# Attention on one Trainium2 core: small sums and multiplies moved from VectorE to GpSimd

## The chip, the cores and the metric

The kernel runs on one core of a Trainium2 chip. The time is that of the whole program on the device, in microseconds (us). The engines are TensorE (PE; its weight loads are PEld), VectorE (DVE), ScalarE (ACT), GpSimd (POOL) and SyncE (SP), which here issues all the transfers (DMA).

## The reference

A layer of a transformer: a normalised input goes through causal attention and then through three blocks of two small linear layers. Masked scores are not left out of the softmax: they count as 1e-10.

```python
x = L0_attn_residual                       # (2, 2048, 256)
# attention of layernorm(x): N = 16 heads, H = 64
scores = einsum('bknh,bqnh->bnqk', keys, queries) / sqrt(H)
scores = where(q_idx < k_idx, 1e-10, scores)
probs = softmax(scores, axis=3)
weighted = einsum('bnqk,bknh->bqnh', probs, values)
x = x + einsum('bqnh,nhe->bqe', weighted, W_output) + Bias_output
# then three times: linear (int4 and low rank), layernorm, gelu, linear, add
x = x + ffn(layernorm(x))
```

## The kernel before, in words

There are three stages with a barrier between them: normalisation and weights, attention, and the feed-forward stage. The change is in attention (function `attention`). Its outer loop runs over N = 16 pairs of heads (two batches, eight pairs each), numbered i = 0 to 15. In a pair the 2048 queries are cut into four groups of 512, worked in the order 3, 2, 1, 0, and a group's keys into tiles of two blocks of 128: NT = 20 tiles in a pair. Group 3 has tiles 0 to 7, group 2 has 8 to 13, group 1 has 14 to 17, group 0 has 18 and 19. For a tile TensorE computes the scores of both heads (`scores`, L822 and L824), ScalarE their exponentials (L961, to `probs`), and TensorE the products with the values (`weighted`, L843, to the PSUM bank `ps_o`). A tile is cut into six slots; between them TensorE does the background work of the next pair: projections (L757), score maxima (L766), and transposes. So 120 slots make a pair (`SLOTS`), and tables of slot numbers say what comes where. Each engine follows its own program in order, and semaphores hold them together.

How a group is finished:
- GpSimd adds up `probs` over the tiles of groups 3, 2 and 1 (`acc`, L724 for a group's first tile, L731 for the others), except in the last pair, where VectorE does that (L1071, L1077). TensorE sums `acc` over the keys with a matrix of ones; ScalarE copies the result to `den_rows` (L926).
- SyncE moves it to 32 partitions (`take_den`, L555, to `den_sq`). VectorE adds the masked keys' part (L1043, `total`) and inverts it (L1047, `inverse`): together they are `invert`.
- SyncE stores the inverse (`put_inverse`, L561) and loads it back spread over the partitions (`spread_inverse`, L570, to `scale`, two transfers).
- GpSimd makes the masked keys' part of the numerator (`masked_part`, L703), VectorE adds it to `ps_o` (`take_numerator`, L1035, to `num`) and multiplies with `scale` (`normalise`, L1055, to `o_out`). SyncE stores the result (`store_heads`, L576).

`num`, `scale` and `o_out` have two buffers, chosen by `group % 2`; `total`, `inverse` and `den_sq` have one. A numerator therefore waits for the multiply that read its buffer before, and TensorE's first product of a group waits for the numerator of the group before:

```python
                    if n >= 2:
                        dve.wait_ge(o_ready, START + n - 1)       # take_numerator
...
                            pe.wait_ge(num_ready, START + 4 * i + (3 - group))   # weighted, first tile of a group
```

Here `n = nth(i, group) = 4 * i + 3 - group` counts the groups. SyncE's queue is written out by hand. It also keeps and installs the split queries and keys of the next pair (`keep_split` L499, `install_chunk` L510, five transfers a chunk) and its maxima (`keep_max` L515, `keep_masked` L531, `install_max` L520). In the stretches below, pair 7 runs from about 1008 to 1127 us, pair 8 follows it, and pair 15 (the last) starts at 1955 us.

## Time and profile before

| | |
|---|---|
| median of 3 runs | 2433.36 us (2431.68 to 2435.09) |
| the profiled execution's own time | 2423.18 us |
| its span, first to last instruction | 2421.4 us |
| mean granted TensorE clock | 0.968 |
| busy: TensorE | 2247.3 us, 93% |
| VectorE | 1421.2 us, 59% |
| GpSimd | 1240.8 us, 51% |
| ScalarE | 813.6 us, 34% |

A busy share is taken over the whole span. An engine that is busy for half of it can still be waited for in one place of each pair, so the shares only say which engine could set the pace; the waits say where it doesn't.

### The profile page before, as it was taken

What the parts mean: (1) busy time and instruction counts of PE and PEld (TensorE: products, weight loads), DVE (VectorE), ACT (ScalarE), POOL (GpSimd) and SP (SyncE); (2) the same over time, 40 slices, a digit from 0 to 9 for tenths busy, and PEclk for the clock granted to TensorE, in tenths of its full rate; (3) what the DMA queues carried; (4) which work ended last, traced back from release to release, by engine and by line L of the source; (5) the groups of instructions that cost most, each with busy time, mean ns of one, the idle gap of its engine ahead of it and who ended that gap; (6) DMA issues with size and microseconds to landing.
All of it is one profiled execution on the core that took longest, in us unless ns stands there. A gap on an engine that the chain in (4) does not pass through costs nothing. (4 is left out here: it accounts for less than half of the span.)

```text
span 2421.4 us, 30652 instructions
## 1 busy us (share of the span) xinstructions
PE 2247.3 (93%) x10080; PEld 1149.0 (47%) x10080; DVE 1421.2 (59%) x3782; ACT 813.6 (34%) x1166; POOL 1240.8 (51%) x1139
## 2 busy tenths in 40 slices
PE   4389999999999999999999999999999995899987
PEld 3224444444444444444444444444444442767764
DVE  3585665656665656565656565656565763265664
ACT  1113434343434343434334344434343442011111
POOL 0106666667676757575757584858584810111110
PEclk8569999999999999999999999999999998899998
DMA  4564363635354445545453536353535332521100
GB/s 122 160 157 108 83 159 80 156 95 140 102 134 111 125 122 147 130 110 134 101 140 95 151 90 152 95 147 99 147 95 141 88 93 73 193 87 61 61 18 18
DMA packets 205356, 273.61 MB, mean 113 GB/s; under 512 B 69201, under 2 KB 86801, under 8 KB 205201
## 3 DMA queue, kind: packets, MB, share of 16 engines
q1 hardware_dynamic: 205200, 271.67, 42.8%
q8 instruction: 82, 1.34, 0.2%
q14 instruction: 74, 0.60, 0.1%
HBM read 176.69 MB, written 94.63 MB: 112 GB/s over the span
## 5 line engine op out<-in xcount | busy, mean ns | idle before, releaser
L731 POOL TENSOR_TENSOR acc<-acc,probs 128x512 f32<-128x512 f32 (+1 forms) x900 | 980.7, 1125 | 377.6 <-ACT probs L961 377.6
L961 ACT ACTIVATE probs<-ps_s 128x1024 f32<-128x1024 f32 (+2 forms) x640 | 549.4, 897 | 332.5 <-PE ps_s L824 157.2
L1011 DVE TENSOR_REDUCE partial<-ps_bg 128x1 f32<-128x512 f32 x768 | 490.3, 684 | 202.8 <-PE ps_bg L766 202.4
L822 PE MATMUL ps_s<-qq,kk 128*128 128x512 f32 (+3 forms) x1280 | 573.2, 448 | 18.8 <-ACT probs L961 18.8
L843 PE MATMUL ps_o<-probs,v 128*64 128x512 f32 (+3 forms) x2560 | 537.8, 541 | 0.0
L824 PE MATMUL ps_s<-qm,kl 128*128 128x512 f32 (+3 forms) x1280 | 467.1, 365 | 0.0
L757 PE MATMUL ps_bg<-xs,w_in 128*128 128x512 f32 x768 | 364.5, 599 | 20.8 <-DMA xs<-xn_turned 18.9
L822 PEld LDWEIGHTS ps_s<-qq,kk 128*128 128x128 f32 x1280 | 243.5, 190 | 202.4 <-issue 154.3
L766 PE MATMUL ps_bg<-k_bf,q_bf 64*128 64x512 bf16 (+3 forms) x1280 | 274.5, 364 | 20.2 <-DVE split L988 10.4
L1008 DVE CUSTOM_DVE_ANT_0 junk<-ps_bg,mask_q 128x512 bf16<-128x512 f32 (+3 forms) x512 | 230.7, 485 | 104.7 <-issue 103.5
L843 PEld LDWEIGHTS ps_o<-probs,v 128*64 128x64 f32 x2560 | 155.3, 136 | 229.9 <-issue 206.0
L824 PEld LDWEIGHTS ps_s<-qm,kl 128*128 128x128 f32 x1280 | 242.5, 189 | 38.8 <-issue 21.5
L766 PEld LDWEIGHTS ps_bg<-k_bf,q_bf 64*128 64x128 bf16 x1280 | 73.6, 93 | 355.0 <-issue 295.1
L910 ACT ACTIVATE split<-ps_bg,bias 128x512 fp32r<-128x512 f32 x128 | 88.0, 688 | 440.8 <-PE ps_bg L757 440.6
L724 POOL TENSOR_TENSOR acc<-probs 128x512 f32<-128x512 f32 x90 | 113.3, 1280 | 237.5 <-ACT probs L961 237.5
L988 DVE SCALAR_TENSOR_TENSOR split<-ps_bg,bias,split 128x512 fp32r<-128x512 f32 x128 | 94.6, 739 | 202.0 <-ACT split L910 201.3
L757 PEld LDWEIGHTS ps_bg<-xs,w_in 128*128 128x128 f32 x768 | 141.6, 191 | 131.0 <-issue 117.5
L1271 POOL TENSOR_TENSOR c_rstd<-c_var,c_minus_half 128x4 f32<-128x4 f32 x32 | 35.2, 1101 | 269.5 <-DVE c_var L1435 269.5
L1304 PE MATMUL c_ps<-c_wo,c_o_in 128*128 128x256 f32 x512 | 114.9, 384 | 28.5 <-DMA c_o_in<-heads_turned 28.5
L703 POOL TENSOR_TENSOR masked_num<-v_from,e 128x512 f32<-128x512 f32 x64 | 76.9, 1201 | 112.5 <-DVE num L1035 110.9
L1304 PEld LDWEIGHTS c_ps<-c_wo,c_o_in 128*128 128x128 f32 x512 | 98.7, 194 | 42.4 <-issue 28.7
L827 PE MATMUL ps_s<-never_above,ident_bf 128*128 128x128 bf16 x512 | 118.0, 230 | 0.0
(102 smaller groups left out, 1659.0 us busy)
## 6 DMA issues: line engine op xcount, KB each, us to landing
high_and_low<-split SPq DMA_DIRECT2D x128, 512.0 KB, 5.8
qq<-high_and_low SPq DMA_DIRECT2D x64, 512.0 KB, 4.7
kk<-high_and_low SPq DMA_DIRECT2D x128, 256.0 KB, 5.5
qm<-high_and_low SPq DMA_DIRECT2D x64, 256.0 KB, 6.4
kl<-high_and_low SPq DMA_DIRECT2D x64, 256.0 KB, 6.8
e<-masked_weights SPq DMA_DIRECT2D x128, 128.0 KB, 3.0
scale<-inverse_sums SPq DMA_DIRECT2D x128, 128.0 KB, 2.9
heads_turned<-o_out SPq DMA_DIRECT2D x64, 256.0 KB, 3.1
```

The source lines that it names most:

```text
L724: g.tensor_tensor(acc[h][:, group % 2, :], pr[:, 0:CH], pr[:, CH:2 * CH], ALU.add).then_inc(added, 1)
L731: g.tensor_tensor(acc[h][:, group % 2, q0:q0 + w], acc[h][:, group % 2, q0:q0 + w], probs[h][:, probs_slot(i, t), at:at + w], ALU.add).the ...
L757: mm = pe.matmul(bank("proj", j, u), w_in[:, s, m, :], xs[:, c, s, :], start=(s == 0), stop=(s == halves - 1))
L766: pe.matmul(bank("max", j, n, h)[:, 0:w], q_bf[HEAD[h], qb * P:(qb + 1) * P], k_bf[HEAD[h], CH * u:CH * u + w], start=True, stop=True).the ...
L822: pe.matmul(out, kk[:, h, kb * P:(kb + 1) * P], qq[:, h, q], start=True, stop=False, skip_group_check=True)
L824: mm = pe.matmul(out, kl[:, h, kb * P:(kb + 1) * P], qm[:, h, q], start=False, stop=not diagonal, skip_group_check=True)
L827: mm = pe.matmul(ps_s[:, h, at:at + P], ident_bf[:, :], never_above[:, :], start=False, stop=True, skip_group_check=True)
L843: mm = pe.matmul(ps_o[64 * h:64 * h + 64, q0:q0 + w], v[:, kb, 64 * h:64 * h + 64], probs[h][:, probs_slot(i, t), at:at + w], start=first, ...
L961: nc.scalar.activation(probs[h][:, probs_slot(i, t), 0:width], ps_s[:, h, 0:width], ACT.Exp, scale=SCORE_SCALE).then_inc(p_ready, 1)
L1008: e.tensor_tensor_reduce(junk[:, k, 0:w], of, mask_q[:, CH - w:CH], 1.0, 3 * NEVER, ALU.add, ALU.max, to).then_inc(max_read, 1)
L1011: e.reduce_max(to, of, AX.X).then_inc(max_read, 1)
L1304: mm = pe.matmul(ps_y[L][:, t, :], o_in[b][:, a, t * P:(t + 1) * P], wo[:, a, :], start=(a == 0 and t % 2 == 0), stop=(a == n_pairs - 1), ...
```

## The change

The sum (`total`) and the multiply (`o_out`) leave VectorE and become GpSimd's, in two functions `total_sum` and `normalise` with the same waits. GpSimd does them between its tiles, by the new tables `TOTAL_TILE` and `NORMAL_TILE`; an entry of NT or more is a tile of the next pair. VectorE keeps the reciprocal, at other slots. SyncE's queue is put in another order around them. The arithmetic is the same.

```diff
-INVERT_SLOT = {3: 68, 2: 106, 1: 118, 0: SLOTS + 8}
-NORMAL_SLOT = {3: 77, 2: 115, 1: SLOTS + 7, 0: SLOTS + 17}
+INVERT_SLOT = {3: 74, 2: 115, 1: SLOTS + 3, 0: SLOTS + 16}
+TOTAL_TILE = {3: 11, 2: 18, 1: NT, 0: NT + 2}
+NORMAL_TILE = {3: 14, 2: NT + 1, 1: NT + 2, 0: NT + 4}
...
+                def total_sum(i, group):
+
+                    n = nth(i, group)
+                    pool.wait_ge(den_sq_in, START + 32 * (n + 1))
+                    pool.wait_ge(masked_den_ready, START + i + 1)
+                    pool.wait_ge(inverse_ready, START + n)
+                    g.tensor_tensor(total[:, :, :], den_sq[:, :, :], masked_den[:, i % 2, group], ALU.add
+                                    ).then_inc(total_ready, 1)
+
+                def normalise(i, group):
+
+                    n = nth(i, group)
+                    pool.wait_ge(scale_in[group % 2], START + 32 * (2 * i + (3 - group) // 2 + 1))
+                    pool.wait_ge(num_ready, START + n + 1)
+                    pool.wait_ge(o_stored[group % 2], START + 16 * (2 * i + (3 - group) // 2))
+                    g.tensor_tensor(o_out[:, group % 2, :], num[:, group % 2, :], scale[:, group % 2, :], ALU.mult
+                                    ).then_inc(o_ready, 1)
+
+                def between_tiles(i, t):
+                    for c in (1, 0):
+                        if i and t == TOTAL_TILE[c] - NT:
+                            total_sum(i - 1, c)
+                    for c in (2, 1, 0):
+                        if i and t == NORMAL_TILE[c] - NT:
+                            normalise(i - 1, c)
+                    for c in (3, 2):
+                        if t == TOTAL_TILE[c]:
+                            total_sum(i, c)
+                    if t == NORMAL_TILE[3]:
+                        normalise(i, 3)
+                    for c in GROUPS:
+                        if t == MASKED_TILE[c]:
+                            masked_part(i, c)
...
                     for t in range(LAST_TILE[1] + 1):
                         group, tile = TILES[t]
-                        for c in (3, 2, 1):
-                            if t == MASKED_TILE[c]:
-                                masked_part(i, c)
+                        between_tiles(i, t)
...
-                    masked_part(i, 0)
-                masked_denominators(N - 1)
-                for c in GROUPS:
-                    masked_part(N - 1, c)
+                    between_tiles(i, LAST_TILE[1] + 1)
+                for t in range(NT):
+                    if t == MASKED_DEN_TILE:
+                        masked_denominators(N - 1)
+                    between_tiles(N - 1, t)
+                for t in range(NT, NT + 5):
+                    between_tiles(N, t - NT)
...
                 def invert(i, group):
 
                     n = nth(i, group)
-                    dve.wait_ge(den_sq_in, START + 32 * (n + 1))
-                    dve.wait_ge(masked_den_ready, START + i + 1)
-                    dve.wait_ge(inverse_ready, START + n)
-                    e.tensor_tensor(total[:, :, :], den_sq[:, :, :], masked_den[:, i % 2, group], ALU.add
-                                    ).then_inc(total_ready, 1)
                     dve.wait_ge(total_ready, START + n + 1)
                     dve.wait_ge(inverse_kept, START + 16 * n)
                     e.reciprocal(inverse[:, :, :], total[:, :, :]).then_inc(inverse_ready, 1)
...
-                normalise(N - 1, 1)
+                invert(N - 1, 1)
                 invert(N - 1, 0)
-                normalise(N - 1, 0)
```

VectorE where one pair ends and the next begins, before. The first row is the reciprocal's neighbour, the multiply of group 2; then come sum and reciprocal of group 1, the numerator of group 0, and the first projection reads of the next pair (`split0`).

```order
L1055 TENSOR_TENSOR o_out<-num,scale 128x512 [waits o_stored0,num_ready,scale_in0]
L1043 TENSOR_TENSOR total<-den_sq,masked_den 32x32 [waits inverse_ready,masked_den_ready,den_sq_in]
L1047 RECIPROCAL inverse<-total 32x32 [waits inverse_kept,total_ready]
L1035 TENSOR_TENSOR num<-ps_o,masked_num 128x512 [waits o_ready,masked_num_ready,pv_done]
L988 SCALAR_TENSOR_TENSOR split0<-ps_bg,bias,split0 128x512 [waits hi_ready]
L994 CAST q_bf<-split0 128x512
L988 SCALAR_TENSOR_TENSOR split0<-ps_bg,bias,split0 128x512 [waits hi_ready]
L996 CAST k_bf<-split0 128x512
```

The same place in the change; the first reciprocal is that of group 2, the second that of group 1.

```order
L1080 RECIPROCAL inverse<-total 32x32 [waits inverse_kept,total_ready]
L1073 TENSOR_TENSOR num<-ps_o,masked_num 128x512 [waits o_ready,masked_num_ready,pv_done]
L1026 SCALAR_TENSOR_TENSOR split0<-ps_bg,bias,split0 128x512 [waits hi_ready]
L1032 CAST q_bf<-split0 128x512
L1080 RECIPROCAL inverse<-total 32x32 [waits inverse_kept,total_ready]
L1026 SCALAR_TENSOR_TENSOR split0<-ps_bg,bias,split0 128x512 [waits hi_ready]
L1034 CAST k_bf<-split0 128x512
```

Each reciprocal has moved one place back in the chain of groups, the sum and the multiply are gone, and the numerator is now ahead of the reciprocal of group 1.

GpSimd at the same place in the change. The first two rows end a pair (the sum of group 2 and the masked part of group 0); the next four stand at tiles 0 and 1 of the next pair (the sum of group 1, the first additions, the multiply of group 2), then come the sum of group 0 and the multiply of group 1 at tile 2. Before, it had only the rows `masked_num` and `acc` here.

```order
L715 TENSOR_TENSOR total<-den_sq,masked_den 32x32
L706 TENSOR_TENSOR masked_num<-v_from,e 128x512
L715 TENSOR_TENSOR total<-den_sq,masked_den 32x32
L759 TENSOR_TENSOR acc<-probs 128x512 x2
L724 TENSOR_TENSOR o_out<-num,scale 128x512
L766 TENSOR_TENSOR acc<-acc,probs 128x512 x4
L715 TENSOR_TENSOR total<-den_sq,masked_den 32x32
L724 TENSOR_TENSOR o_out<-num,scale 128x512
L766 TENSOR_TENSOR acc<-acc,probs 128x512 x2
```

The sum of group 1 now stands ahead of the next pair's first additions, and the multiply of group 2 behind them.

SyncE over the same stretch, before. `den_sq` is `take_den` of group 1; the inverse behind it is that of group 1, and the five transfers from `high_and_low` ahead of it install chunk 1.

```order
L510 DMA qq<-high_and_low 128x2x512
L510 DMA kk<-high_and_low 64x2x512 x2
L510 DMA qm<-high_and_low 64x2x512
L510 DMA kl<-high_and_low 64x2x512
L555 DMA den_sq<-den_rows 32x1x16 x2
L576 DMA heads_turned<-o_out 128x512
L515 DMA maxima<-rows 8x128
L531 DMA masked_weights<-rows 8x128
L561 DMA inverse_sums<-inverse 32x2x16
L520 DMA qm<-maxima 1x2x512
L515 DMA maxima<-rows 8x128
L531 DMA masked_weights<-rows 8x128
```

The same stretch in the change. The inverse and the spread are those of group 2, `den_sq` is group 1's.

```order
L511 DMA qq<-high_and_low 128x2x512
L511 DMA kk<-high_and_low 64x2x512 x2
L511 DMA qm<-high_and_low 64x2x512
L511 DMA kl<-high_and_low 64x2x512
L516 DMA maxima<-rows 8x128
L532 DMA masked_weights<-rows 8x128
L562 DMA inverse_sums<-inverse 32x2x16
L571 DMA scale<-inverse_sums 64x512 x2
L556 DMA den_sq<-den_rows 32x1x16 x2
L521 DMA qm<-maxima 1x2x512
L516 DMA maxima<-rows 8x128
L532 DMA masked_weights<-rows 8x128
```

The denominators of group 1 have moved behind the maxima and masked weights of the next pair's group 1, and behind the inverse of group 2 and its spread, which stood ahead of the five transfers before.

## Rows read from the trace of the kernel before

**Rows 1.** The page, part 1: busy us, share of the span, instructions

```profile
PE 2247.3 (93%) x10080; PEld 1149.0 (47%) x10080; DVE 1421.2 (59%) x3782; ACT 813.6 (34%) x1166; POOL 1240.8 (51%) x1139
```

**Rows 2.** Chain of waits, TensorE, 297 to 1955: total us, times, longest

```profile
PE ps_s L822 <- ACT probs L961: 16.2, 14, 1.2
PE ps_bg L766 <- DVE split L988: 9.7, 14, 0.7
PE ps_bg L757 <- DVE split L988: 1.7, 5, 0.5
```

**Rows 3.** Timeline, ScalarE (start, us): first exponential of pairs 0, 1, 15

```profile
178.84 1.06 ACT L961 ACTIVATE probs<-ps_s 128x1024 f32<-128x1024 f32 x1
...
297.01 1.02 ACT L961 ACTIVATE probs<-ps_s 128x1024 f32<-128x1024 f32 x1
...
1955.47 1.02 ACT L961 ACTIVATE probs<-ps_s 128x1024 f32<-128x1024 f32 x1
```

**Rows 4.** Timeline, four engines, end of pair 7, start of 8; [idle before]

```profile
1123.59 0.40 ACT L935 ACTIVATE rows<-rows,masked_bias 8x128 f32<-8x128 f32 x1
...
1122.27 0.69 DVE L1055 TENSOR_TENSOR o_out<-num,scale 128x512 f32<-128x512 f32 x1
1129.26 0.79 DVE L1043 TENSOR_TENSOR total<-den_sq,masked_den 32x32 f32<-32x32 f32 x1 [6.30 <-DMA den_sq<-den_rows]
...
1130.36 0.62 DVE L1035 TENSOR_TENSOR num<-ps_o,masked_num 128x512 f32<-128x512 f32 x1
...
1131.74 0.42 DVE L994 CAST q_bf<-split 128x512 bf16<-128x512 f32 x1
...
1128.74 2.53 POOL L724 TENSOR_TENSOR acc<-probs 128x512 f32<-128x512 f32 x2 [9.51 <-ACT probs L961]
...
1133.79 1.51 PE L843 MATMUL ps_o<-probs,v 128*64 128x512 f32 x6
```

**Rows 5.** Timeline, SyncE's queue, the same place

```profile
1122.12 1.20 SPq L555 DMA_DIRECT2D den_sq<-den_rows  x2
...
1124.36 0.30 SPq L531 DMA_DIRECT2D masked_weights<-rows  x1
```

**Rows 6.** Timeline, SyncE's queue, end of the last pair

```profile
2026.66 0.31 SPq L561 DMA_DIRECT2D inverse_sums<-inverse  x1
2028.02 1.12 SPq L570 DMA_DIRECT2D scale<-inverse_sums  x2
2029.26 1.17 SPq L555 DMA_DIRECT2D den_sq<-den_rows  x2
```

**Rows 7.** The line L555 in the stretch 2026 to 2032

```profile
DMA to landing us min/median/max: 1.9/2.1/2.2
```

**Rows 8.** GpSimd by form, 297 to 1955: busy us, mean ns, idle before

```profile
L731 POOL TENSOR_TENSOR acc<-acc,probs 128x256 f32<-128x256 f32 x84 | 61.8, 757 | 0.0
L731 POOL TENSOR_TENSOR acc<-acc,probs 128x128 f32<-128x128 f32 x84 | 37.2, 465 | 0.0
```

**Rows 9.** Timeline, VectorE and TensorE, tile 2 of pair 8

```profile
1143.19 0.18 DVE L1043 TENSOR_TENSOR total<-den_sq,masked_den 32x32 f32<-32x32 f32 x1 [3.57 <-DMA den_sq<-den_rows]
...
1144.24 1.22 DVE L994 CAST q_bf<-split 128x512 bf16<-128x512 f32 x1
...
1144.37 1.98 PE L757 MATMUL ps_bg<-xs,w_in 128*128 128x512 f32 x4 [0.17 <-DVE split L988]
```

**Rows 10.** Timeline, TensorE, last pair: first product, and tile 5

```profile
1959.09 1.08 PE L843 MATMUL ps_o<-probs,v 128*64 128x512 f32 x4
...
1980.01 0.50 PE L822 MATMUL ps_s<-qq,kk 128*128 128x512 f32 x1 [1.02 <-ACT probs L961]
```

**Rows 11.** Timeline, SyncE's queue and VectorE, end of attention

```profile
2039.05 0.35 SPq L561 DMA_DIRECT2D inverse_sums<-inverse  x1
...
2045.01 0.34 SPq L576 DMA_DIRECT2D heads_turned<-o_out  x1
...
2044.28 0.69 DVE L1055 TENSOR_TENSOR o_out<-num,scale 128x512 f32<-128x512 f32 x1 [5.26 <-DMA scale<-inverse_sums]
```

More of the change, by code:

```diff
@@ L607, in _ @@
                     if i:
-                        spread_inverse(i - 1, 0)
+                        store_heads(i - 1, 1)
                     if more:
                         keep_split(i + 1, 2)
+                    if i:
+                        put_inverse(i - 1, 0)
+                        spread_inverse(i - 1, 0)
                     spread_masked(i, 2)
+                    if more:
+                        keep_split(i + 1, 1)
                     if i:
@@ L636, in _ @@
                         install_chunk(i + 1, 2)
+                    store_heads(i, 3)
+                    if more:
                         keep_max(i + 1, 2, fin_before(i, fin_index("mt", 2)) + 1)
@@ L641, in _ @@
                         install_max(i + 1, 2)
+                        install_chunk(i + 1, 1)
+                        keep_max(i + 1, 1, fin_before(i, fin_index("mt", 1)) + 1)
+                        keep_masked(i + 1, 1)
                     put_inverse(i, 2)
                     spread_inverse(i, 2)
[L644 to L645 removed]
                     take_den(i, 1)
[L647 to L651 removed]
                     if more:
@@ L1108, in _ @@
                                 invert(i - 1, g)
-                            if i and n == NORMAL_SLOT[g] - SLOTS:
-                                normalise(i - 1, g)
                         for g in GROUPS:
```

33 lines of the change are left out of this document (8 added, 25 removed).

## The prediction

> **What bounds the kernel now.** I read the page first: TensorE is busy 93% of the span [rows 1], and the part of the span in which it is not is mostly the first stage and the turn to the last one. The change is in the attention stage, so the next view is the chain of waits, cut to that stage: of some 1,658 us (pairs 1 to 14) TensorE waits 16.2 us for ScalarE's exponentials, 9.7 us for VectorE in front of a maxima product and 1.7 us for VectorE in front of a projection [rows 2]. The reader is to see two things there. First, TensorE sets the pace: whatever another engine saves is worth at most what TensorE waits for it. Second, the first two waits come 14 times each, once a pair, and are hand-overs TensorE, ScalarE, (VectorE), TensorE in which nothing of the change takes part. Then I took the length of a pair from ScalarE's timeline: pair 0 runs from 178.84 to 297.01, 118.17 us, and pairs 1 to 14 from 297.01 to 1955.47, 118.46 us each [rows 3]. Pair 0 has no earlier pair whose sums and divisions are finished in it; so what that finishing costs TensorE now is 118.46 - 118.17 = 0.29 us a pair.
>
> **Where the 0.29 us is.** In tile 2 VectorE waits 3.57 us for the denominators of group 0, adds them late, and only then reads the projection bank; TensorE's next projection waits for that read [rows 9]. The wait shown is 0.17 us in this pair; it is longer where the transfer is later.
>
> **The change, part by part.**
> (1) VectorE loses 64 sums and 64 multiplies. VectorE is idle before both now (6.30 us before the sum in [rows 4]), so the work saved is worth nothing by itself. What counts is that it no longer stands in a wait for a transfer at slot 8 of the pair: the bank read of tile 2 gets free. Worth up to 0.29 us, 14 times: -4.1 us. I take all of it, since the reciprocal stands at slot 16 now, behind the work that TensorE waits for. The other end is nothing, if the reciprocals wait for GpSimd instead.
>
> (2) GpSimd gains four sums and four multiplies a pair. They lie between its accumulations, and a late accumulation holds up ScalarE three tiles later, a long way off: GpSimd idles 9.51 us before it starts a pair [rows 4], and its extra work is some 4 x (0.35 + 1.26) = 6.4 us in 118. No term.
>
> (3) The new wait. The numerator of group 0, the last of a pair, goes to the buffer of group 2, so its instruction (L1035) waits until group 2 has been multiplied. Before, that multiply stood on VectorE at 1122.27, long done [rows 4]. Now it is GpSimd's, at tile 1 of the next pair, behind the sum for group 1 and behind the two additions of tile 0. TensorE's first product with the values in the new pair waits for this numerator, because it overwrites the PSUM bank, and it starts at 1133.79 now [rows 4]. Queued behind the numerator on VectorE are the first two projection reads. I follow the new chain in the times of that pair:
> - SyncE issues the inverse of group 2 behind the masked weights of group 1, which are ready at 1123.59 + 0.40 = 1123.99 [rows 4]; with that issue (about 0.4 us from one small one to the next) 1124.4 [rows 5]. The inverse itself has long been computed.
> - From that issue to the landing of group 1's denominators: the tail of the kernel has the same row of issues without anything else in flight. Inverse at 2026.66, two spreads from 2028.02, denominators at 2029.26 and about 2029.8 [rows 6], 1.9 to 2.2 us to land [rows 7], so 2031.8: 5.1 us. They land at 1129.5, near where they land now (1129.26 [rows 4]), since five large transfers no longer stand right ahead of them.
> - GpSimd's sum of 32x32 has no row. Below, the line through 757 ns for 256 columns and 465 ns for 128 [rows 8] gives 465 - 96 x 2.28 = 246 ns; above, it costs no more than 465 ns. I take 0.35: 1129.85.
> - Two additions, 2.53 us [rows 4]: 1132.4. Today they start at 1128.74; they can't before the sum now.
> - The multiply at the price of one such addition, 1.26 us: 1133.65. The numerator 0.62 us [rows 4]: 1134.3. Three hand-overs, 0.2 us in all: 1134.5.
> TensorE is ready at 1133.79, so it waits 0.7 us, at 14 boundaries: +9.8 us. The ends: sum at 0.25, the landing 0.2 earlier and no hand-over cost give 0.2 us; sum at 0.46 and the landing 0.5 later give 1.3 us. Times 14, +3 to +18.
>
> [...]
>
> (4) The last pair has no projections, so TensorE is at its first product already 3.6 us after the pair's start, at 1959.09 [rows 10]. Denominators land 2.8 us after the start (1955.47 [rows 3]), at 1958.3; sum 0.35, multiply 1.26 (no additions ahead of it, VectorE does them there), numerator 0.62, hand-overs 0.2: 1960.7, +1.6 us. Against it, TensorE waits 1.02 us in tile 5 today because VectorE's additions stood behind a wait for denominators and one for the inverse [rows 10]; both leave VectorE or come earlier: -1.0. Together +0.6.
>
> (5) The end of attention is a serial chain. The inverse of group 2 is issued 0.8 us later (2027.5 for 2026.66 [rows 6]), as its reciprocal now stands behind the numerator of group 1. Then 5.1 us to the next denominators, 0.35 + 1.26 + 0.62 + 0.34 for sum, multiply, numerator and reciprocal, with hand-overs 2035.3; the same 5.1 and 0.35 + 0.34 to 2041.1; from there to the last multiply 5.2 us (2039.05 to 2044.28 [rows 11]) and 1.26 for it: the last store at 2047.6 for 2045.01 [rows 11]. +2.6 us, and nothing hides it, since the last stage starts after it.
>
> **The sum:** -4.1 + 9.8 + 0.6 + 2.6 = +8.9 us, on the profiled execution's 2423.2 us: 2432.1. That execution lies 10.2 us under the median of the runs, 2433.36; the difference is added to the median: 2442.3, so 2442.
>
> **The rivals.**
> - *The new wait hides* (chance 0.14; the side that is not slower). If the numerator is done by 1133.79, that is if the chain is 0.7 us shorter than I make it, TensorE never waits. For it: the margin is small, and the chain was put together from rows of other places. Against: five of its links are rows, and it starts at a ScalarE instruction that the change can't move. Then -4.1 + 0.6 + 2.6 = -0.9 us: 2432, no change that can be measured. It decides at a landing of 1128.8.
> - *The chain is longer* (0.08): the spreads or denominators share their queues with the chunk's five transfers that follow, or the sum costs GpSimd 1 us. At 1.7 us a boundary, 14 x 1.0 more: 2456.
> - *VectorE and GpSimd get in each other's way* (0.05). VectorE's cast in tile 2 takes 1.22 us beside GpSimd's additions [rows 9] and 0.42 at 1131.74 [rows 4] without them, and its sum 0.79 us at 1129.26 beside them. Every multiply on GpSimd is a new stretch of this. If one of the four in a pair falls on a cast ahead of a read that TensorE waits for, 14 x 0.8 = 11 us more: 2453. The Trainium skill (SBUF — State Buffer, SBUF: two separate sides) says that the two share a port pair which one instruction holds to its end; by that rule it would be so, and these rows agree. But the multiplies at the boundary fall where VectorE stands still anyhow.
> - *VectorE's relief is worth more* (0.03): if it also ended the 9.7 us of [rows 2], about 2423. Against it: these waits come at one place in each pair, behind a projection that ScalarE has just read.
> - The forecast has what is left, 0.70.
>
> **The numbers.** With the forecast's ends (+3 to +18 for the boundary term, nothing to -4.1 for the first) its own range is 2435 to 2454. The range 2433 to 2456 leaves out most of the no-wait case (0.14) and the last rival, and takes in the longer ones. 0.2%, 4.9 us, is about what a measurement of this kernel can tell from no change. Slower by more than that: 0.64 of the forecast and the two longer cases, 0.77; within it: the hidden wait, and 0.05 of the forecast's lower edge, 0.19; faster, the last rival and a hundredth of the forecast, 0.04.
>
> **What would show it.** In the changed profile: the chain of waits has a new one, TensorE's product with the values (out ps_o) for VectorE's numerator, 15 times, 0.7 us each and 1.6 in the last pair. VectorE idles before the numerator until GpSimd's multiply. GpSimd's sum of 32x32 is at 0.25 to 0.46 us and starts 2.8 us after the pair's start. TensorE's waits for VectorE before a projection (1.7 us now) are gone. Pairs 1 to 14 are 118.9 us long. The last store is issued about 3 us later than now, counted from the last pair's start (89.54 us now [rows 3, 11]). I am wrong if the product with the values starts at once in a new pair; or if pairs lengthen with no wait at that product, which would speak for the shared port or a transfer.

## The result, and the profile after

| | before | changed |
|---|---|---|
| median, both timed side by side | 2434.23 us (4 runs, 2431.68 to 2444.36) | 2472.70 us (4 runs, 2466.16 to 2488.62) |
| profiled execution: span | 2421.4 us | 2476.6 us |
| pairs 1 to 14 in it | 1658.46 us | 1697.79 us |

The ratio is 1.016, with a 95% interval of 1.0099 to 1.022: slower, by 38.5 us, some four times the 8.9 us that were forecast (2442, range 2433 to 2456). The direction was right and the range too low.

The changed profile's page, engine line. GpSimd is busy for 1339.1 us where it was 1240.8, VectorE for 1393.0 where it was 1421.2; both have idle time to spare, so the shares explain nothing.

```profile
PE 2271.4 (92%) x10080; PEld 1163.5 (47%) x10080; DVE 1393.0 (56%) x3654; ACT 814.0 (33%) x1166; POOL 1339.1 (54%) x1267
```

ScalarE's timeline of the changed kernel at the starts of pairs 0, 1 and 15, as in [rows 3] (columns: start, duration, then what it is).

```profile
189.25 1.03 ACT L999 ACTIVATE probs<-ps_s 128x1024 f32<-128x1024 f32 x1
...
307.38 1.02 ACT L999 ACTIVATE probs<-ps_s 128x1024 f32<-128x1024 f32 x1
...
2005.17 1.02 ACT L999 ACTIVATE probs<-ps_s 128x1024 f32<-128x1024 f32 x1
```

The span grew by 55.2 us. The stage ahead of pair 0 took 10.4 us longer (189.25 for 178.84). That is not the change's: in the other profiles below, of either kernel, it begins at anything from 176.2 to 188.8. Pair 0, which finishes no earlier pair, is as long as before (118.13 us for 118.17). Pairs 1 to 14 are 39.3 us longer. The last store is issued 92.40 us after the start of pair 15, 2.9 later than before, and 2.6 us lie behind it. What lies behind the last store varies by as much among the profiles of this document (376.2 to 379.6 us). So I count 42 us as the change's. From ScalarE's exponentials one also reads each tile's length; over pairs 1 to 14 the mean changed so:

| tile | before, us | changed, us | times 14 |
|---|---|---|---|
| 1 | 7.61 | 8.36 | +10.5 |
| 2 | 4.73 | 4.47 | -3.6 |
| 3 | 10.30 | 12.03 | +24.2 |
| 4 | 7.99 | 8.19 | +2.9 |
| 5 | 5.26 | 5.59 | +4.6 |
| others | | | +0.8 |

Tile 3 is not a little longer everywhere: it is 10.30 us in nine of these pairs and 14.42, 17.27, 12.63, 14.66 and 16.69 us in pairs 3, 5, 8, 11 and 13. The same stretch in TensorE's waits of the changed kernel (waited for: us in total, times, longest), to be laid beside [rows 2]:

```profile
PE ps_bg L804 <- DVE split L1026: 9.7, 14, 0.7
PE ps_o L881 <- DVE num L1073: 9.5, 14, 1.2
PE ps_bg L795 <- DVE partial L1046: 9.4, 2, 4.7
PE ps_bg L804 <- DVE vt L1021: 6.0, 3, 2.2
PE ps_bg L804 <- DVE partial L1049: 4.5, 7, 1.0
PE ps_bg L804 <- DVE partial L1046: 2.0, 4, 0.6
```

The second row is the forecast wait for the numerator. The third and fourth were in nobody's list: two plus three waits in five pairs, for bank reads of VectorE that have nothing to do with the change. The fifth row lies in tile 5 of other pairs, and comes below. What VectorE did there, pair 5, timeline of VectorE and of GpSimd, with TensorE's wait:

```profile
806.12 0.75 DVE L1026 SCALAR_TENSOR_TENSOR split<-ps_bg,bias,split 128x512 fp32r<-128x512 f32 x1 [3.24 <-ACT split L948]
806.78 8.00 DVE L1032 CAST q_bf<-split 128x512 bf16<-128x512 f32 x1
814.71 0.68 DVE L1046 CUSTOM_DVE_ANT_0 junk<-ps_bg,mask_q 128x512 bf16<-128x512 f32 x1
...
806.48 0.24 POOL L715 TENSOR_TENSOR total<-den_sq,masked_den 32x32 f32<-32x32 f32 x1 [0.71 <-DMA den_sq<-den_rows]
806.69 1.26 POOL L724 TENSOR_TENSOR o_out<-num,scale 128x512 f32<-128x512 f32 x1
807.92 6.58 POOL L766 TENSOR_TENSOR acc<-acc,probs 128x512 f32<-128x512 f32 x8
...
815.45 2.08 PE L795 MATMUL ps_bg<-xs,w_in 128*128 128x512 f32 x2 [4.72 <-DVE partial L1046]
```

The cast shows as 8.00 us, as against 0.42 alone. It ends 0.3 us after GpSimd's row of ten instructions does (807.92 + 6.58 = 814.50), and behind it stand the reads that TensorE waits for. In pair 6 GpSimd paused 0.63 us between multiply and additions, and the same cast took 0.65:

```profile
932.13 0.24 POOL L715 TENSOR_TENSOR total<-den_sq,masked_den 32x32 f32<-32x32 f32 x1
932.34 1.28 POOL L724 TENSOR_TENSOR o_out<-num,scale 128x512 f32<-128x512 f32 x1
934.25 6.78 POOL L766 TENSOR_TENSOR acc<-acc,probs 128x512 f32<-128x512 f32 x8 [0.63 <-ACT probs L999]
...
933.26 0.65 DVE L1032 CAST q_bf<-split 128x512 bf16<-128x512 f32 x1
```

In the kernel before, no cast took more than 1.33 us: it waited for one GpSimd instruction at most. I call it a *hold* when a VectorE instruction stands through several.

Which of pairs 1 to 14 have one can be read off. In the five with a hold, the exponentials for which the additions wait end 0.22 to 1.30 us before the multiply ahead of them does, so the additions stand ready. In eight pairs they end after it, GpSimd pauses 0.09 to 0.63 us, and nothing is held. Pair 7 lies between: ready 0.13 us early (1052.34 + 1.71 = 1054.05, the multiply ends at 1054.18), no pause to be seen, and yet the cast gets in after one boundary:

```profile
1052.34 1.71 ACT L999 ACTIVATE probs<-ps_s 128x896 f32<-128x896 f32 x2
...
1053.14 1.33 DVE L1032 CAST q_bf<-split 128x512 bf16<-128x512 f32 x1
...
1052.71 0.24 POOL L715 TENSOR_TENSOR total<-den_sq,masked_den 32x32 f32<-32x32 f32 x1 [0.74 <-DMA den_sq<-den_rows]
1052.92 1.26 POOL L724 TENSOR_TENSOR o_out<-num,scale 128x512 f32<-128x512 f32 x1
1054.15 6.97 POOL L766 TENSOR_TENSOR acc<-acc,probs 128x512 f32<-128x512 f32 x8
```

A hold costs TensorE more than its wait. In tiles 3 and 4 the waits behind held casts sum to some 17 us (the third and fourth rows above, and 0.5 us each in tile 4 of pairs 3, 5 and 11), but the two tiles are 27.1 us longer. TensorE's granted clock, at its full level (1.0, 2.4 GHz) through pairs 1 to 14 of the kernel before, falls to the lower one (0.5, 1.2 GHz) in five stretches here, 20.5 us in all, in four of the five pairs with a hold. In pair 5 TensorE had stood still for all but 0.01 us of the 4.72 ahead of 815.45; in pair 11 for 2.21 us ahead of 1542.51. Two of the five stretches (columns: stretch, its length, busy time of PE, PEld, DVE, ACT and POOL, granted clock, DMA):

```profile
812.97:819.79 6.82, 4.34 (x8) 1.47 (x10) 4.56 (x10) 0.00 (x0) 1.52 (x4) 0.50 0.43 116
1543.42:1546.83 3.41, 3.41 (x7) 1.67 (x5) 0.88 (x7) 0.00 (x0) 0.00 (x0) 0.50 0.65 193
```

TensorE is busy for 17.6 of these 20.5 us. At full clock that work would take about half, so I estimate 8.8 us for the clock; about 1 of the 27.1 us is left over.

Tile 5 is another matter. It is at 5.26 or 5.27 us in the five pairs with a hold, and up to 6.29 in the others: there VectorE's cast waits for one GpSimd instruction, as in [rows 9], and TensorE's next maxima product waits for the reads behind it (the fifth row of the waits). In the kernel before that cast took 0.42 us in every pair; now the multiply of group 0 at tile 4 puts GpSimd's next instructions beside it (runs 14 and 15, with that multiply on GpSimd and no hold there, show the longer tile 5 too). Pair 6:

```profile
956.02 1.44 DVE L1032 CAST q_bf<-split 128x512 bf16<-128x512 f32 x1
...
955.90 1.27 POOL L706 TENSOR_TENSOR masked_num<-v_from,e 128x512 f32<-128x512 f32 x1
957.22 3.81 POOL L766 TENSOR_TENSOR acc<-acc,probs 128x512 f32<-128x512 f32 x3
```

The first account of the holds was: any longer unbroken run of GpSimd can hold a cast (theory A); the rival was a late transfer or the numerator's wait, carried on.

### The profile page after: what moved, and what is told of

The parts are those of the page before. It is cut to its first block and busy times, and to the rows that moved or that the text cites. A ratio compares the mean times of both kernels' runs of the same rounds, so it can differ in the third digit from the quotient of the medians.

```text
span 2476.6 us, 30652 instructions
## 1 busy us (share of the span) xinstructions
PE 2271.4 (92%) x10080; PEld 1163.5 (47%) x10080; DVE 1393.0 (56%) x3654; ACT 814.0 (33%) x1166; POOL 1339.1 (54%) x1267
## 3 DMA queue, kind: packets, MB, share of 16 engines
q8 instruction: 82, 1.34, 0.2%
## 5 line engine op out<-in xcount | busy, mean ns | idle before, releaser
L860 PE MATMUL ps_s<-qq,kk 128*128 128x512 f32 (+3 forms) x1280 | 574.2, 449 | 17.6 <-ACT probs L999 17.6
L795 PE MATMUL ps_bg<-xs,w_in 128*128 128x512 f32 x768 | 372.8, 611 | 27.9 <-DMA xs<-xn_turned 18.5
L804 PE MATMUL ps_bg<-k_bf,q_bf 64*128 64x512 bf16 (+3 forms) x1280 | 275.7, 364 | 33.1 <-DVE split L1026 10.4
L862 PEld LDWEIGHTS ps_s<-qm,kl 128*128 128x128 f32 x1280 | 242.6, 190 | 39.3 <-issue 22.1
L724 POOL TENSOR_TENSOR o_out<-num,scale 128x512 f32<-128x512 f32 x64 | 82.2, 1284 | 170.1 <-DMA scale<-inverse_sums 170.0
L1073 DVE TENSOR_TENSOR num<-ps_o,masked_num 128x512 f32<-128x512 f32 x64 | 43.9, 686 | 178.3 <-POOL o_out L724 171.6
L715 POOL TENSOR_TENSOR total<-den_sq,masked_den 32x32 f32<-32x32 f32 x64 | 15.7, 245 | 231.7 <-DMA den_sq<-den_rows 231.4
```

The costliest lines, as they stand in the source:

```text
L795: mm = pe.matmul(bank("proj", j, u), w_in[:, s, m, :], xs[:, c, s, :], start=(s == 0), stop=(s == halves - 1))
L804: pe.matmul(bank("max", j, n, h)[:, 0:w], q_bf[HEAD[h], qb * P:(qb + 1) * P], k_bf[HEAD[h], CH * u:CH * u + w], start=True, stop=True).the ...
L860: pe.matmul(out, kk[:, h, kb * P:(kb + 1) * P], qq[:, h, q], start=True, stop=False, skip_group_check=True)
L862: mm = pe.matmul(out, kl[:, h, kb * P:(kb + 1) * P], qm[:, h, q], start=False, stop=not diagonal, skip_group_check=True)
```

## The experiments

Pairs 1 to 14 are from the profiled execution of each; medians compare with the kernel before on the same chip. Runs 7 to 11, 16 and 17 were executed once each and the kernel of run 5 twice: for them the profile's tiles and casts count, not the time.

**1. Multiply of group 2 ahead of tile 0's additions.**

```diff
-NORMAL_TILE = {3: 14, 2: NT + 1, 1: NT + 2, 0: NT + 4}
+NORMAL_TILE = {3: 14, 2: NT, 1: NT + 2, 0: NT + 4}
```

> The changed kernel, but GpSimd multiplies group 2 ahead of its additions of tile 0 of the next pair instead of behind them (one entry of the table of multiplies, NT for NT + 1). Both theories agree on the first part: TensorE's wait at the first product with the values (for VectorE's numerator; 9.5 us over 14 pairs, longest 1.2) is gone or under 2 us, tile 1 of a pair is back from 8.34 to about 7.6 us. Theory A (most of the loss is VectorE's cast standing through a run of GpSimd instructions in tiles 2 and 3, 24 us in five of 14 pairs): the long tile 3 stays, pairs 1 to 14 are 10 us shorter, about 2463. Rival B (everything comes from the new wait, which delays what follows it): pairs 1 to 14 go back to 1660 us or so, 2435 to 2440.

Median 2483.27 us (before 2426.20), ratio 1.0235 (1.018 to 1.0289); pairs 1 to 14: 1711.3 us. Tile 1 is 7.61 us in all pairs: that wait was the multiply's place, as forecast. But holds of 4.1 to 8.2 us are now in 12 of 14 pairs. Rival B is out; A is right in kind and too small in size. More pairs are hit because in more of them the additions of tile 2 stand ready early: 0.32 to 1.40 us before the multiply ahead of them ends in the 12 pairs with a hold, 0.12 and 0.06 us in the two without. Here 41 us of pairs 1 to 14 are at the lower clock.

**2. The cast as another instruction.**

```diff
-e.tensor_copy(q_bf[:, cols(c)], part[:, 0, :].bitcast(F32))
+e.reduce_max(q_bf[:, cols(c)], part[:, 0, :].bitcast(F32).unsqueeze(2), AX.X)
```

> The changed kernel, but VectorE's two casts of the split queries and keys (0.42 us each when nothing disturbs them, 8.00 and 7.95 us in pairs 5 and 13 of the changed kernel, 4.2 to 4.6 in pairs 3, 8 and 11) are done by another instruction with the same result, a maximum over an axis of one element. Theory A (the cast is an instruction that needs something which GpSimd's additions hold, and it can stand through several of them): no such instruction takes over 1.3 us, tile 3 is back at 10.3 us in all pairs, tile 5 at 5.3; pairs 1 to 14 take 1697.8 - 24 - 4 = about 1670 us, with up to 5 us more if the other form itself costs 0.3 us at each of its 8 places; about 2445 us. Rival B (the long tiles come from late transfers that the cast only shows, since it stands behind them): the waits turn up on another instruction of VectorE and the time stays at 2465 to 2475.

Median 2444.69, ratio 1.0087 (1.0055 to 1.0118); pairs 1 to 14: 1676.5 us, tile 3 at 10.30 in all. VectorE's rows for the two casts as maxima (min/median/max ns): not one of 128 was touched (662 to 678 ns).

```profile
L1032 DVE TENSOR_REDUCE q_bf<-split x64: 674/676/678, 110.1 to 1892.9; 128x512 bf16<-128x512 f32 x64
L1034 DVE TENSOR_REDUCE k_bf<-split x64: 662/675/677, 111.4 to 1898.4; 128x512 bf16<-128x512 f32 x64
```

So the hold belongs to the instruction, not to what it waits for. The dearer form costs 0.26 us in each of tiles 4 and 5, the same in every pair: the single-boundary waits of tile 5 are gone too.

**3 and 4. One unused multiply put into the kernel before**, ahead of tile 2's additions, behind the wait for both exponentials (3) or for the first (4).

```diff
+if t == 2:
+    pool.wait_ge(p_ready, START + 2 * NT * i + 2 * t + 1)   # run 4; run 3 stands behind the full wait
+    g.tensor_tensor(idle_out[:, :], mask_q[:, :], mask_q[:, :], ALU.mult).then_inc(idle_done, 1)
```

> The kernel before with one instruction added on GpSimd in tile 2 of every pair but the last: a 128x512 multiply of constants whose result nobody uses (so the outputs are those of before). It stands behind GpSimd's wait for the exponentials of tile 2, directly ahead of the additions of that tile, and nothing else moves, no transfer either. Theory A1 (any longer back-to-back run of GpSimd can hold VectorE's cast for long): some casts over 2 us, TensorE stands in tile 3 of some pairs, pairs 1 to 14 longer by 3 to 25 us. Theory A2 (the cast is held only when GpSimd never stood still, that is when its additions were ready while the instruction ahead of them still ran): as the additions follow without a gap here too, a cast that begins beside this multiply can be held as well; one that begins later waits for one addition as before. Rival B (late transfers are the cause): nothing over 1.33 us, the time of before within 0.2%.

> The kernel before with the same unused 128x512 multiply on GpSimd in tile 2, but behind the first head's exponential of that tile alone, ahead of the wait for both heads: it starts some 0.5 us earlier, while the second head's exponential is still being computed, as the group's multiply often did in the changed kernel. Theory A (GpSimd's longer runs hold the cast): casts of 4 to 8 us in several of 14 pairs and a tile 3 of 12 us or more in these, pairs 1 to 14 longer by 10 to 30 us, about 2445 to 2460. Rival B (late transfers): no cast over 1.33 us, the time of before within 0.2%.

Ratios 1.0003 (0.9976 to 1.0029) and 1.0015 (0.9992 to 1.0038); no cast over 1.27 us. Theory A as stated falls: a longer unbroken run, as long as these, is not enough.

**5 and 6. A 32x32 sum and a multiply; two multiplies**, unused, at the same place.

```diff
+g.tensor_tensor(idle_sum[:, :, :], <32x32 of mask_q>, <32x32 of mask_q>, ALU.add).then_inc(idle_done, 1)   # run 5
+g.tensor_tensor(idle_out[:, 0, :], mask_q[:, :], mask_q[:, :], ALU.mult).then_inc(idle_done, 1)            # 5; twice in 6
```

> The kernel before with two unused instructions on GpSimd in tile 2 of every pair but the last, ahead of that tile's additions: a 32x32 sum and, straight behind it, a 128x512 multiply, of constants, into buffers that nobody reads. They start after the first head's exponential of the tile, so the additions follow without a gap, as in pairs 3, 5, 8, 11 and 13 of the changed kernel. Nothing else moves. The multiply alone at this place held no cast over 1.3 us. Theory A (it takes the small sum in front, or a run of at least two instructions in front of the additions): casts of 4 or 8 us in several pairs, tile 3 of 12 us or more there, pairs 1 to 14 longer by 10 to 35 us, 2435 to 2460. Rival B (the changed order of the transfers is needed as well): no cast over 1.6 us, the time of before within 0.2%.

> As the run with an unused sum and multiply, but with two unused 128x512 multiplies, no small sum: the same number of instructions in the run. Theory A3 (the number of instructions ready in a row counts): long casts as with sum and multiply. Theory A4 (the short instruction on 32 partitions counts, as the next instruction stands ready behind it at once): no cast over 1.6 us here. If neither this nor the run with the sum shows a long cast, both fall.

With the sum: ratio 1.0314 (1.0269 to 1.0359), pairs 1 to 14 at 1750.8 us, a hold in every one of pairs 0 to 14, and 79 us of pairs 1 to 14 at TensorE's lower clock. With two multiplies: 0.9993 (0.9967 to 1.0019), none. So SyncE's new order isn't needed for a hold, and at this place the sum is. In pair 4 of run 5 it is VectorE's own small sum that is held, 4.96 us for 0.18, until GpSimd has nothing more to do (689.35 + 4.37 = 693.72):

```profile
688.80 4.96 DVE L1054 TENSOR_TENSOR total<-den_sq,masked_den 32x32 f32<-32x32 f32 x1 [4.24 <-DMA den_sq<-den_rows]
...
688.14 0.24 POOL L722 TENSOR_TENSOR idle_sum<-mask_q 32x32 f32<-32x32 f32 x1 [1.23 <-ACT probs L972]
688.35 1.03 POOL L725 TENSOR_TENSOR idle_out<-mask_q 128x512 f32<-128x512 f32 x1
689.35 4.37 POOL L742 TENSOR_TENSOR acc<-acc,probs 128x512 f32<-128x512 f32 x4
```

**7 to 11. What it is about the sum.** Each is run 5 with its unused instructions changed. Run 7 has the sum alone, behind the wait for both exponentials; runs 8, 9 and 10 have these in place of the 32x32 sum; run 11 has the 32x32 sum alone, behind the first exponential, so that GpSimd then pauses for the second.

```diff
+g.tensor_tensor(idle_out[:, 1, 0:32], mask_q[:, 0:32], mask_q[:, 32:64], ALU.add)             # run 8, 128x32
+g.tensor_tensor(idle_out[0:32, 1, :], mask_q[0:32, :], mask_q[0:32, :], ALU.add)              # run 9, 32x512
+g.tensor_tensor(idle_out[0:64, 1, 0:32], mask_q[0:64, 0:32], mask_q[0:64, 32:64], ALU.add)    # run 10, 64x32
```

> The kernel before with one unused 32x32 sum on GpSimd, directly ahead of the additions of tile 2 and released with them, so that they follow it without a gap; no multiply. Theory A5 (the short instruction in front of a run is what makes the run hold VectorE to its end): long casts or a long sum of denominators on VectorE, 4 to 8 us, in several pairs; pairs 1 to 14 over 1680 us. Theory A6 (a short instruction and a long one must stand ahead of the additions): nothing over 1.6 us, pairs 1 to 14 at 1657 to 1662 us.

> As the run with an unused 32x32 sum and a multiply in the kernel before (which took 1751 us for pairs 1 to 14 and showed holds of 3.9 to 7.5 us in most pairs), but the sum is as short on all 128 partitions (128x32). If shortness is the cause, the holds stay, 1720 to 1770 us. If it is that the sum uses 32 partitions only, they vanish, 1657 to 1670 us.

> The opposite case: the sum is on 32 partitions but 512 elements long, some 1.0 us like the multiply behind it. If shortness is the cause of the holds: nothing over 1.6 us, pairs 1 to 14 at 1657 to 1670 us. If the use of 32 partitions is: holds in most pairs, over 1700 us.

> As the runs with an unused short sum and a multiply ahead of tile 2's additions in the kernel before, but the sum on 64 partitions. With 32 partitions pairs 1 to 14 took 1751 us, with 128 they took 1662. If every sum on fewer than all 128 partitions does it: over 1700 us and casts of 4 to 7 us; if 64 are enough to be harmless: 1657 to 1665.

> The kernel before with the one unused 32x32 sum, released by the first head's exponential of tile 2 and so ahead of the additions with a pause of some 0.4 us between them. The sum released with the additions, without a pause, held VectorE 3.7 to 6.8 us in 12 pairs and took 1728 us for pairs 1 to 14. If a moment in which GpSimd stands still undoes it: no cast over 1.6 us, 1657 to 1662 us. If not: over 1700.

| the unused instructions ahead of tile 2's additions | pairs 1 to 14, us | pairs of 0 to 14 with a VectorE cast or sum over 1.6 us (longest) |
|---|---|---|
| 32x32, multiply | 1750.8 | 15 (7.46) |
| 32x32 alone | 1727.9 | 15 (6.81) |
| 64x32, multiply | 1744.9 | 15 (7.69) |
| 128x32, multiply | 1661.9 | none |
| 32x512, multiply | 1671.6 | 5 (3.31) |
| 32x32, pause, additions | 1665.8 | none |
| two multiplies | 1667.2 | none |

Shortness alone is not it: 128x32 is as short (252 ns) and harmless. Using fewer than all partitions is, whether 32 or 64, and mostly when the instruction is short as well; with 512 elements the holds are few and end after two or three additions, which neither theory gave. A pause undoes it. The few us over 1658 of the harmless ones are in tile 2, where VectorE's sum waits for denominators that land later than before, and in some pairs for one GpSimd instruction (up to 1.16 us in all).

The kernel before has a GpSimd instruction on 32 partitions too (L694, 32x128, the fifth of its run). It says nothing either way: no cast or two-input sum of VectorE falls into the 4.9 us of the run behind it.

**12. The sum of the changed kernel on 128 partitions.** 96 of them hold a constant that nobody reads on, filled in once at the start.

```diff
-        total = sb("total", [32, 2, 16])     # den_sq and masked_den alike
+        total = sb("total", [P, 2, 16])
```

> The changed kernel with its sum of denominators done on 128 partitions instead of 32 (96 of them hold a constant that nobody reads on; the sum is as short, and no instruction, wait or transfer changes its place). Theory P (GpSimd's instruction on 32 partitions in front of its run is what holds VectorE): no cast over 1.6 us in tiles 2 and 3 of any pair, tile 3 at 10.3 us in all; the wait at the numerator stays (9.5 us over 14 pairs), so pairs 1 to 14 take 1697.8 - 24 to 28 = 1670 to 1674 us and the run about 2447. Rival (it is the place in the run or the changed order of transfers, and the unused instructions in the kernel before only happened to look alike): some pairs keep a tile 3 of 12 to 17 us, over 1685.

Median 2445.88, ratio 1.0049 (1.0027 to 1.0072); pairs 1 to 14 at 1677.7 us, tile 3 at 10.30 in all. VectorE's cast and GpSimd's run of pair 5, same place, same neighbours:

```profile
791.55 1.41 DVE L1034 CAST q_bf<-split 128x512 bf16<-128x512 f32 x1
...
791.19 0.25 POOL L717 TENSOR_TENSOR total<-den_sq,masked_den 128x32 f32<-128x32 f32 x1 [0.75 <-DMA den_sq<-den_rows]
791.40 1.28 POOL L726 TENSOR_TENSOR o_out<-num,scale 128x512 f32<-128x512 f32 x1
792.63 6.97 POOL L768 TENSOR_TENSOR acc<-acc,probs 128x512 f32<-128x512 f32 x8
```

The additions were ready 0.21 us early in this pair, which is next to the margin of pair 7 above; but they were 0.64, 0.84 and 1.27 us early in pairs 13, 8 and 3, and no cast of the run took over 1.52 us. This is the cause of the holds shown in the change itself. Against the changed kernel tiles 3 and 4 are 27 us shorter, but tile 1 is 4 us longer over 14 pairs (in pair 11 it takes 11.79 us: the numerator's longest wait, 2.4 us, and then 3.4 us at the lower clock), and tile 5 is 4 us longer, since more pairs reach it with the single-boundary wait. That is why the run is 4 us over the expectation.

**13. The same with run 1's table.**

> The same with the multiply of group 2 ahead of the additions of tile 0: both faults of the change mended, all sums and multiplies still on GpSimd at their tiles. Without the wide sum this order was the worse one (1711 us in pairs 1 to 14, long casts in 12 of 14). Theory P: tiles 1, 2, 3 at 7.61, 4.47, 10.3 us in every pair, some tenths lost in tile 5, pairs 1 to 14 at 1656 to 1661 us, about 2432 with the longer tail. Rival: over 1685.

Median 2433.07, ratio 0.9992 (0.9968 to 1.0016); pairs 1 to 14 at 1661.8 us. The order that was worst with a 32-partition sum is level with before when the sum is wide.

**14. The narrow sum moved to where GpSimd then pauses.**

```diff
-INVERT_SLOT = {3: 74, 2: 115, 1: SLOTS + 3, 0: SLOTS + 16}
-TOTAL_TILE = {3: 11, 2: 18, 1: NT, 0: NT + 2}
-NORMAL_TILE = {3: 14, 2: NT + 1, 1: NT + 2, 0: NT + 4}
+INVERT_SLOT = {3: 74, 2: 115, 1: SLOTS + 3, 0: SLOTS + 18}
+TOTAL_TILE = {3: 11, 2: 18, 1: NT, 0: NT + 4}
+NORMAL_TILE = {3: 14, 2: NT, 1: NT + 2, 0: NT + 5}
...
+                normalise(N - 1, 0)
```

> The changed kernel with GpSimd's work at other tiles: sum of group 0 ahead of tile 4 instead of tile 2 (there GpSimd then stands still), its reciprocal two slots later, its multiply at tile 5, and the multiply of group 2 ahead of the additions of tile 0. The multiply of group 1 stays ahead of tile 2's additions, now without a sum in front. Theory A (a short sum ahead of a long run is what costs): no cast over 1.6 us in tiles 2 and 3, tile 3 at 10.3 us, tile 1 at 7.6, tile 2 at 4.47; pairs 1 to 14 at 1655 to 1660 us; 5 us of the last pair and the tail remain, so 2425 to 2432, within 0.3% of before. Rival: the run moves elsewhere and holds another cast, over 1670 us in pairs 1 to 14.

Median 2430.91, ratio 1.0003 (0.998 to 1.0025); pairs 1 to 14 at 1661.8 us, no hold. Tile 5 is 5.77 us for 5.26 in each pair, behind the multiply of group 0.

**15. Only the multiplies on GpSimd**, the sum back in `invert`, at the changed slots.

```diff
 def invert(i, group):
+    e.tensor_tensor(total[:, :, :], den_sq[:, :, :], masked_den[:, i % 2, group], ALU.add).then_inc(total_ready, 1)
```

> The changed kernel with the sum of denominators back on VectorE, ahead of its reciprocal at the changed kernel's slots; the multiply stays on GpSimd and SyncE's order stays. Theory A4 (the small sum in GpSimd's run is needed for the long casts): no cast over 1.6 us, tile 3 at 10.3 us; the new wait at the first product with the values stays (9.5 us or somewhat less, as the multiply of group 2 no longer has a sum ahead of it, perhaps 3); pairs 1 to 14 at 1662 to 1672, total 2430 to 2440. Theory A3 (any longer run does it): with the multiply of group 1 still ahead of the additions of tile 2, long casts in some pairs, total over 2450. VectorE's sum for group 1 at slot 3 may wait for the denominators, at 2.8 us into the pair, and costs nothing there.

Median 2500.40, ratio 1.0254 (1.0216 to 1.0291), pairs 1 to 14 at 1724.1 us where I expected 1662 to 1672. Tiles 1, 2 and 3 are 7.61, 4.47, 10.30: no hold there. But tile 13 is 7.77 for 4.12 and tile 14 6.21 for 5.38. Of its VectorE sums one in each of pairs 0 to 14 (that of group 3) took 3.7 us:

```profile
L1066 DVE TENSOR_TENSOR total<-den_sq,masked_den x64: 154/174/3729, 270.4 to 2120.0; 32x32 f32<-32x32 f32 x64
```

No instruction on fewer partitions stands in GpSimd's run there. There is a second way into a hold.

**16 and 17. The kernel before, with that sum at the late slot; and a cast ahead of it.**

```diff
-INVERT_SLOT = {3: 68, 2: 106, 1: 118, 0: SLOTS + 8}
-NORMAL_SLOT = {3: 77, 2: 115, 1: SLOTS + 7, 0: SLOTS + 17}
+INVERT_SLOT = {3: 74, 2: 106, 1: 118, 0: SLOTS + 8}
+NORMAL_SLOT = {3: 86, 2: 115, 1: SLOTS + 7, 0: SLOTS + 17}
+                        if n == 68:                                     # run 17 alone
+                            e.tensor_copy(idle_bf[:, :], mask_q[:, :]).then_inc(idle_done, 1)
```

> The kernel before with sum and reciprocal of group 3 on VectorE at slot 74 instead of 68, where the run with the multiplies alone on GpSimd had them, and its multiply at slot 86 instead of 77, so that it doesn't wait for its transfer. GpSimd's program is untouched. In that other run this sum stood 3.73 us in every pair, until GpSimd's run ended, with no 32-partition instruction in the run since GpSimd last stood still; in the kernel before the same sum, six slots earlier in the same run, stood 1.10 us (to the next boundary). Theory L (it is enough that VectorE asks late in a long run, whose last stillness of GpSimd was some 19 us ago): the sum takes 3.7 us here too, tile 13 is about 7.7 us instead of 4.12, pairs 1 to 14 about 1708 us. Rival (GpSimd's changed program or the transfers made it so there): 0.4 to 1.3 us for the sum, pairs 1 to 14 at 1658 to 1662.

> The same, with one unused 128x512 cast on VectorE at slot 68, where the sum stood in the kernel before (its result is read by nobody). Theory L1 (the run of GpSimd gets out of step over time, and one VectorE instruction that gets in between two of its instructions puts it in step again): the unused cast takes 1 to 1.5 us and the sum at slot 74 no more than 1.3 us, pairs 1 to 14 at 1658 to 1665. Theory L2 (what stands nearest to the sum decides, whatever came before): the sum takes 3.7 us as in the run without the cast.

Run 16: pairs 1 to 14 at 1733.1 us, tile 13 at 7.70. That tile is as theory L said, the total 25 us over it: TensorE waits 2.66 us behind the held sum, then 3.4 or 6.8 us of every pair are at the lower clock, which reaches into tile 14 (6.53 us for 5.38), and tile 2 is longer too. VectorE and GpSimd in pair 7; GpSimd starts the run after a pause of 3.56 us, and 19 us later its 16th instruction since is under way:

```profile
1137.02 3.73 DVE L1043 TENSOR_TENSOR total<-den_sq,masked_den 32x32 f32<-32x32 f32 x1
...
1118.22 9.94 POOL L731 TENSOR_TENSOR acc<-acc,probs 128x512 f32<-128x512 f32 x8 [3.56 <-ACT probs L961]
1128.12 1.09 POOL L703 TENSOR_TENSOR masked_num<-v_from,e 128x512 f32<-128x512 f32 x1
1129.16 11.54 POOL L731 TENSOR_TENSOR acc<-acc,probs 128x512 f32<-128x512 f32 x12
```

Run 17: the sum takes 0.78 us in that pair, tile 13 is 4.22 us and pairs 1 to 14 take 1673.5 us; 10 of the 15 us over the kernel before are tile 2. The cast took 1.34 us in pairs 1 to 14, and 8.11 in pair 0, where it was held itself. L and L1 are borne out: a long run holds by itself, and a VectorE instruction that got in between undoes it for what follows. But the run's age alone doesn't decide: the cast of pair 0 asked 12.45 us into the run and was held, those of pairs 1 to 14 at 12.42 us and got in, as did the sum of the kernel before at 12.42 to 12.45. What else differs isn't shown.

**18. The one part of the change that paid, alone:** the kernel before with `INVERT_SLOT[0]` at `SLOTS + 10`.

> The kernel before with one entry changed: sum and reciprocal of group 0 on VectorE two slots later (10 for 8 in the next pair), behind the bank read of tile 2. If the first term of the prediction holds without the rest of the change, tile 2 is 4.47 us long instead of 4.73, pairs 1 to 14 take 1654.8 instead of 1658.4 us, and the time falls by 3.7 us, 0.15%, which the timing alone can hardly tell from nothing. Rival: the wait for the late denominators moves to the read of tile 3, and nothing or less than 1 us is won.

Tile 2 is 4.47 us in all pairs, pairs 1 to 14 take 1654.8 us, and TensorE's waits for VectorE in front of a projection are gone. Median 2422.96 (before 2436.11), ratio 0.9946 (0.9925 to 0.9968), 12 and 23 runs. It beats both kernels. The profile accounts for 3.6 us, 0.15%. The 0.5% of the timing are more than that; the runs of before in that set spread from 2424.8 to 2449.3, and its medians in the other sets of several runs lie between 2426.2 and 2435.2, so I would count on the 3.6.

## Why the prediction was wrong

- *Term 1, VectorE's relief, -4.1 us.* Right: -3.6 (tile 2), and again -3.65 alone (run 18).
- *Term 3, the new wait, +9.8.* Right in place, number and size: 9.5 us, 14 times; tile 1 +10.5. In pair 8 of the changed kernel GpSimd sums at 1158.17, 2.77 us after the pair's start (forecast 2.8), for 0.24 us (forecast 0.25 to 0.46); its additions take 2.50, the multiply 1.26, and the numerator 0.69 at 1162.24. Run 1 takes the wait away by the multiply's place.
- *Terms 4 and 5, last pair and tail, +0.6 and +2.6.* The last store was forecast about 3 us later, counted from the last pair's start; it is 2.9. The last pair is 0.6 us longer up to its last exponential, and the wait at its first product is 1.6 us, as forecast.
- *Term 2, GpSimd's extra work, "No term".* This is the step that failed, and it is most of the miss: +24.2 us in tile 3, +2.9 in tile 4 and +4.6 in tile 5, 31.7 us where nothing was put. I judged the new work by GpSimd's slack for its own products, not by what else stands still while it runs.
- It was a rival (*VectorE and GpSimd get in each other's way*), with the right pair of engines and the wrong price and chance. I took 0.8 us for a collision from [rows 9], where the cast had waited for one instruction. That is the price of one boundary, and it fits tile 5: 4.6 us, of the 11 that the rival put there. A hold lasts for the run, 4 to 8 us, and the lower clock behind it was in no term and no rival: some 9 of the 27 us of tiles 3 and 4. And "the multiplies at the boundary fall where VectorE stands still anyhow" was true of tile 0, but sum of group 0 and multiply of group 1 fall into tile 2, beside the cast of [rows 9] itself. The rival's sum, 2453, stopped short because nothing in the trace of before shows a hold; none happened there.
- The rule quoted with it, of the Trainium skill (SBUF — State Buffer, SBUF: two separate sides), is that one instruction has the shared port pair for its whole length while the other engine is blocked. The casts of the trace of before agree (1.33 us at most). I read it as a bound of one instruction on the wait, and that reading fails in the changed kernel: 8.00 us through nine.
- The terms that I named sum to +8.9; with the holds in tiles 3 and 4 the sum is 36, and with tile 5 some 41, against 42 measured.

What is shown and what is not: shown are three things that change whether VectorE gets in between two GpSimd instructions: an instruction on 32 or 64 partitions at the head of the run (runs 5, 7, 10 against 6, 8, 12), a later place in a long run (16), and what undoes it, a pause (11) or a VectorE instruction that got in (17). They don't settle every case: pair 7 of the changed kernel and pairs 1 and 2 of run 1 have the narrow head and a pause of 0.02 us or none to be seen, and no hold; pair 0 of run 17 has one that its neighbours haven't. One reading of all of them is that GpSimd's partitions fall out of step, so that some are always at work and no moment is left at which VectorE may have what both use; a narrow instruction puts them out of step at once, a long run slowly. That is argued, not shown; no trace here shows GpSimd's partitions apart. Why a 32x512 instruction does less harm than a 32x32 one stays open too.

## What to carry to other kernels

Before moving small work to an engine with idle time, list what the other engines do beside its new place, not only who waits for it. Where a kernel looks like this one, look for VectorE casts and two-input sums beside unbroken GpSimd runs: keep narrow GpSimd instructions out of the head of a long run (put them before a pause, or widen them to all 128 partitions), or give VectorE an instruction that isn't held, as the maximum in place of the cast in run 2. And a wait seen at one length is a lower bound: price it by the run that could hold it, not by the one instruction that happened to. Where TensorE sets the pace, add what its clock does behind the wait: in pair 11 a wait of 2.21 us was followed by 3.4 us at the lower clock.

## What the runs showed of the hardware that I had not expected

- A VectorE cast of 0.42 us stood up to 8.18 us through up to ten GpSimd instructions (run 1), a 32x32 sum of 0.18 us up to 5.5 (run 10); a maximum from SBUF into bf16 was never touched (662 to 678 ns), nor was VectorE's reciprocal (314 to 343 ns in all runs).
- TensorE's granted clock went from 1.0 to 0.5 with four of the five holds of the changed kernel, for 3.4 or 6.8 us, and once more in tile 4 of pair 11; in the kernel before it stayed at 1.0 from 177 to 2038 us.
- In the kernel before, its sum of group 3 at slot 68 waits for one boundary (1.1 us); at slot 74 tiles 13 and 14 are 66 us longer over 14 pairs (7.70 and 6.53 us for 4.12 and 5.38). The table lay six slots from a cliff that its own profile doesn't show.
- GpSimd's 32x32 sum takes 0.24 us, its 128x32 one 0.25, its 32x512 one 1.03, as much as a 128x512 multiply of the same operand: its time goes by the length, not by the partitions.
